# Block softmax attention: scores of both heads as float32 matmuls in the two row halves of the PE array, in rounds of two score tiles

## What is computed

```python
scale = D ** (-0.5)
q = (x @ Wq).reshape(B, S, H, D).transpose(0, 2, 1, 3)     # H = 16, D = 64
k, v = ...                                                 # the same with Wk, Wv
def step(carry, kv):                                       # over blocks of 64 keys
    o, m, l = carry
    kj, vj = kv
    s = jnp.einsum('bhnqd,bhkd->bhnqk', qb, kj) * scale
    m_new = jnp.maximum(m, s.max(axis=-1))
    p = jnp.exp(s - m_new[..., None])
    alpha = jnp.exp(m - m_new)
    l_new = alpha * l + p.sum(axis=-1)
    o_new = (alpha[..., None] * o + jnp.einsum('bhnqk,bhkd->bhnqd', p, vj)) / l_new[..., None]
    return ((o_new, m_new, l_new), None)
out = o.transpose(0, 2, 1, 3).reshape(B, S, H * D) @ Wo
x = x + out
```

## Time and profile before

| | |
|---|---|
| median of 3 runs | 3036.59 us |
| lowest, highest | 3035.76, 3037.22 us |
| the profiled execution: its time | 3035.88 us |
| its span in the trace | 3031.6 us |
| busy over the span: PE, DVE, ACT, POOL | 80%, 76%, 52%, 44% |
| the softmax attention, first projection to last addition | about 762 to 2552 us |

### The profile page before, as it was taken

One profiled execution on the slowest core, in us unless ns is written; L12 is line 12 of the kernel. 1 busy time (PEld: TensorE's weight loads), 2 busy tenths in 40 slices (PEclk: granted clock), 3 DMA queues, 4 the chain that ended last, 5 costly groups with the idle time before them and its releaser, 6 DMA issues. The chain is left out here.

```text
span 3031.6 us, 44901 instructions
## 1 busy us (share of the span) xinstructions
PE 2417.3 (80%) x15028; PEld 1802.3 (59%) x15028; DVE 2307.4 (76%) x4330; ACT 1571.3 (52%) x2571; POOL 1325.7 (44%) x893
## 2 busy tenths in 40 slices
PE   4985149951599999999999999999999996229980
PEld 2443148840377777777777777777777775218860
DVE  4535537754599999999998999999999996817762
ACT  2432123321377777777777777777777774113330
POOL 0001721135255555555555555555555554541117
PEclk8986579985699999999999999999999998559995
DMA  4240136642422323323233232232322310026652
GB/s 112 104 173 13 38 118 193 192 127 66 99 71 66 89 52 76 79 66 89 52 72 84 60 89 58 66 89 58 88 62 66 89 43 3 24 86 193 192 160 77
DMA packets 158617, 267.91 MB, mean 88 GB/s; under 512 B 30945, under 2 KB 105313, under 8 KB 158433
## 3 DMA queue, kind: packets, MB, share of 16 engines
q1 hardware_dynamic: 144048, 231.84, 28.9%
q0 software_dynamic: 8192, 16.79, 1.8%
q10 hardware_dynamic: 6192, 16.91, 1.4%
HBM read 120.83 MB, written 46.07 MB: 55 GB/s over the span
## 5 line engine op out<-in xcount | busy, mean ns | idle before, releaser
L1513 POOL TENSOR_TENSOR b_prob<-b_prob,b_weight 128x1024 f32<-128x1024 f32 x512 | 958.9, 1905 | 837.4 <-DVE b_weight L1489 837.4
L1452 DVE TENSOR_REDUCE b_bmax<-b_score 128x16 f32<-128x1024 f32 x512 | 621.4, 1214 | 89.7 <-PE b_score L1327 85.7
L1413 ACT ACTIVATE b_prob<-b_score,b_neg_m 128x1024 f32<-128x1024 f32 x512 | 570.9, 1115 | 170.5 <-DVE b_neg_m L1462 169.6
L1439 DVE TENSOR_REDUCE b_bsum<-b_prob 128x16 f32<-128x1024 f32 x512 | 618.8, 1209 | 0.0
L1403 ACT ACTIVATE b_pT<-b_turn 128x512 f32<-128x512 f32 x1024 | 555.4, 597 | 63.2 <-PE b_turn L1338 52.8
L1338 PE MATMUL b_turn<-ident,b_prob 128*128 128x128 f32 x4096 | 531.3, 273 | 1.0 <-ACT b_pT L1403 1.0
L1338 PEld LDWEIGHTS b_turn<-ident,b_prob 128*128 128x128 f32 x4096 | 477.8, 140 | 72.2 <-issue 3.2
L1327 PE MATMUL b_score<-b_KH,b_QS 128*128 128x512 f32 x1024 | 492.4, 481 | 23.4 <-issue 8.2
L1307 PE MATMUL b_acc<-b_pT,b_V 128*64 128x256 f32 x4096 | 498.5, 385 | 0.0
L1327 PE MATMUL b_score<-b_KL,b_QS 128*128 128x512 f32 x1024 | 406.0, 396 | 0.0
L1307 PEld LDWEIGHTS b_acc<-b_pT,b_V 128*64 128x64 f32 x4096 | 271.2, 136 | 154.0 <-issue 43.1
(11 more groups left out here) (196 smaller groups left out, 2706.9 us busy)
## 6 DMA issues: line engine op xcount, KB each, us to landing
f_e_w<-f_weights SPq DMA_DIRECT2D x80, 776.0 KB, 4.3
b_KH<-b_k_high SPq DMA_DIRECT2D x128, 256.0 KB, 4.4
b_KL<-b_k_low SPq DMA_DIRECT2D x128, 256.0 KB, 4.8
f_sorted<-a_zero ACTq DMA_DIRECT2D x43, 384.0 KB, 4.5
b_hb<-b_hT SPq DMA_DIRECT2D x32, 512.0 KB, 5.0
b_QS<-b_q_high SPq DMA_DIRECT2D x64, 256.0 KB, 3.5
b_QS<-b_q_low SPq DMA_DIRECT2D x64, 256.0 KB, 4.1
f_e_z<-f_sorted SPq DMA_DIRECT2D x82, 128.0 KB, 4.1
```

The source lines that it names most:

```text
L1413: act.activation(prob[r % 4][k][:], score[k % 2][:], ACT.Exp, bias=neg_m[r % 2][:, k:k + 1]).then_inc(prob_ready, 1)
L1439: dve.tensor_reduce(bsum[r % 2][:, k, :], prob[r % 4][k][:].rearrange("p (n c) -> p n c", c=KV_BLOCK), AX, ALU.add).then_inc(sum_ready, 1)
L1452: maxima = chain.mark(dve.tensor_reduce(bmax[r % 2][:, k, :], score[k % 2][:].rearrange("p (n c) -> p n c", c=KV_BLOCK), AX, ALU.max))
L1513: pool.tensor_tensor(tile, tile, weight[r % 2][:, k, :].unsqueeze(2).to_broadcast([P, NB, KV_BLOCK]), ALU.mult).then_inc(scaled, 1)
```

## The change

The scores become plain float32 matmuls with 64 rows: head 0 in partitions 0 to 63 and head 1 in 64 to 127, straight from the projection's own layout. So the split in high and low parts, its DVE instruction, the 12 DMAs of each pair and their semaphores go; ACT's copy of a projection (`qk_copy`) writes Q or K directly. The stream of each engine is no longer by tile but by **round** of two tiles (both heads of one query tile), rd = 0 and 1 in a slot:

```diff
+        Q = [sb(f"Q{i}", [P, SEQ]) for i in range(2)]
+        K = [sb(f"K{i}", [P, SEQ]) for i in range(2)]
+        def projected(j, r, rd, scores):
+            n, i = 2 * (r % GPP) + rd, 2 * j + r // GPP + 1
+            if not scores or i == PAIRS:
+                return None
+            if 1 <= n <= 4:
+                return "qk", i, i % 2, n - 1
+            if n >= 6:
+                return "v", i, i % 2, n - 6
+            return None
```

```diff
 PE
-                            if not (isinstance(sl, int) and sl == 0 and k < 2):
-                                pe.wait_ge(prob_ready, 4 * sl + k - 1)
-                            for c in range(2):
-                                for n, Kx in enumerate((KH, KL)):
-                                    last = pe.matmul(score[k % 2][:, c * HALF:(c + 1) * HALF], QS[par][h][:, q * P:(q + 1) * P],
-                                                     Kx[par][h][:, c * HALF:(c + 1) * HALF], start=n == 0, stop=n == 1)
-                            last.then_inc(scored, 1)
+                def score_round(j, r, rd):
+                    sl, par, q = 8 * j + r, r // GPP, (r % GPP) * QT + rd
+                    if rd == 0:
+                        pe.wait_ge(qk_taken, 4 * (2 * j + par) + 4)
+                    if sl or rd:
+                        pe.wait_ge(prob_ready, 4 * sl + 2 * rd)
+                    for c in range(2):
+                        for h in range(2):
+                            mine = slice(h * HD, (h + 1) * HD)
+                            last = pe.matmul(score[h][:, c * HALF:(c + 1) * HALF], Q[par][mine, q * P:(q + 1) * P],
+                                             K[par][mine, c * HALF:(c + 1) * HALF], start=True, stop=True)
+                    last.then_inc(scored, 2)
+                    for rd in range(2):
+                            score_round(j, r, rd)
+                        if rd == 1 and before:
+                            out_proj(g - 1, (gr - 1) % 8)
+                            turn_probs(g, gr, 2 * rd)
+                        if rd == 0 and before:
+                            pv(g - 1, (gr - 1) % 8, 2)
+                            pv(g - 1, (gr - 1) % 8, 3)
+                        if rd == 1 and finish:
+                            pv(g, gr, 0)
+                            pv(g, gr, 1)
+                        if finish:
+                            turn_probs(g, gr, 2 * rd + 1)
+                        made = projected(j, r, rd, scores)
```

```diff
 ACT, each round: oT copy (rd 1), two pT copies, two exponentials, two pT copies, rise (rd 0), projection copy
+                            for h in range(2):
+                                k = 2 * rd + h
+                                act.wait_ge(max_ready, 4 * sl + k + 1)
+                                act.activation(prob[r % 4][k][:], score[h][:], ACT.Exp,
+                                               bias=neg_m[r % 2][:, k:k + 1]).then_inc(prob_ready, 1)
 DVE
+                def maxima(sl, r, k):
+                    chain.link(dve.tensor_reduce(bmax[r % 2][:, k, :], score[k % 2][:].rearrange("p (n c) -> p n c", c=KV_BLOCK), AX, ALU.max))
+                    dve.tensor_reduce(neg_m[r % 2][:, k:k + 1], bmax[r % 2][:, k, :], AX, ALU.max, negate=True).then_inc(max_ready, 1)
+                    for rd in range(2):
+                            dve.wait_ge(scored, 4 * sl + 2 * rd + 2)
+                            for h in range(2):
+                                maxima(sl, r, 2 * rd + h)
+                        if rd == 0 and rest:
                             block_sums(n, nr, GT - 1)
+                            chain.link(dve.tensor_tensor_scan(flat(run_max), flat(first_low), flat(bmax[nr % 2]), 0.0, ALU.add, ALU.max))
...
+                        if rd == 0 and scores:
+                            block_sums(sl, r, 0)
...
+                        if rd == 1 and scores:
+                            block_sums(sl, r, 1)
+                            block_sums(sl, r, 2)
-                        made = projected(j, r, k, scores)
-                        if made and made[0] == "qk":
-                            low(made[1], made[3])
```

More of the change, by code:

```diff
@@ L1312, in slot, with out_proj @@
+                def out_proj(g, gr):
+                    misc_free()
+                    pe.wait_ge(o_ready, g + 1)
+                    hp = (g // GPP) % (HEADS // 2)
+                    for q in range(QT):
+                        last = pe.matmul(misc[:, q * D:(q + 1) * D], oT[gr % 2][:, q * P:(q + 1) * P], wo[:, hp, :],
+                                         start=True, stop=True)
+                    last.then_inc(wo_done, 1)
+                    last_use[0] = (wo_taken, g + 1)
                 def slot(j, r, scores, finish):
-                    sl, par = 8 * j + r, r // GPP
@@ L1445, in slot @@
-                    first = isinstance(sl, int) and sl == 0
-                    before = not (isinstance(sl, int) and sl <= LAG)
-                    rest = not first and (scores or r == 0)
+                    g, gr, before = sl - LAG, (r - LAG) % 8, sl > LAG
+                    rest = sl > 0 and (scores or r == 0)
                     n, nr = sl - 1, (r - 1) % 8
-                    for k in range(GT):
+                    for rd in range(2):
                         if scores:
-                            dve.wait_ge(scored, 4 * sl + k + 1)
-                            maxima = chain.mark(dve.tensor_reduce(bmax[r % 2][:, k, :], score[k % 2][:].rearrange("p (n c) -> p n c", c=KV_BLOCK), AX, ALU.max))
-                        if k == 0 and rest:
-                            m_i = chain.mark(dve.tensor_tensor_scan(flat(run_max), flat(first_low), flat(bmax[nr % 2]), 0.0, ALU.add, ALU.max))
-                        if k == 1 and rest:
-                            dve.wait_ge(rise_ready, n + 1)
-                            chain.wait(sums)
-                            scaled_sums = chain.mark(dve.tensor_tensor(flat(inv_l), flat(rise), flat(run_sum), ALU.mult))
-                        if scores:
-                            chain.wait(maxima)
-                            dve.tensor_reduce(neg_m[r % 2][:, k:k + 1], bmax[r % 2][:, k, :], AX, ALU.max, negate=True).then_inc(max_ready, 1)
-                        if k == 0 and rest:
@@ L1500, in _ @@
                 chain.link(dve.memset(last_one[:, :, NB - 1:NB], 1.0))
-                for u in range(4):
-                    low(0, u)
                 slots(dve, slot)
```

182 lines of the change are left out of this document (56 added, 126 removed).

## The result

The changed kernel takes 3074.85 us (median of 4 runs, 3073.34 to 3077.90) against 3036.47 for the kernel before on the same chip: a ratio of 1.0128 (95% interval 1.0110 to 1.0145), 38 us slower. The forecast was 3058, with 3022 to 3112 as its range and slower at 0.75. The profiled execution took 3074.61 us, of which its span is 3070.7, against 3031.6 before: 39.1 us to account for.

The account below looks back on a forecast made before the run. A DVE and POOL loop with the scan held in every slot was to bound it, with some PE lateness. Slots (13.80 - 13.57) x 127 = +29.2, start -9.3, end +2: +21.9, so 3058 us; range 3022 to 3112.

Parts of the forecast that it names:

- The loop of DVE and POOL: Weight, POOL, held scan, rest of DVE's stream, next weight: a floor of 13.7 us in all four slots.
- held until POOL is through: DVE's scan with two SBUF inputs waits for POOL's four multiplications, ending 0.14 us later, 8.00 us after the weight.
- PE late behind ACT's copy: PE's Wo product waits for ACT's copy of the V product: 0.1 to 0.2 us added in two slots of four.
- A score round: On PE, four matmuls with row halves side by side: 2.05 us, against 2.02 for two tiles before.
- B: PE's row halves run side by side but not freely: 0.3 to 0.5 us more a round, 3084 to 3121; chance 0.13.
- C: PE's row halves don't run together: 1.64 us more each round, slot about 16.7, 3426 us; chance 0.06.
- The start: Before the first scores: no deal and no low-part instructions, -9.8, less 0.5 for the exponential table: -9.3 us.
- the exponential table: At the start, the table would then be late, taking 0.5 us off the gain.
- The end: Last slots without scores do the same work; 2 us added for the last slot's longer chain.
- Rival D: DVE's scan isn't held for long, only PE binds: slot 13.2 to 13.3, 2989 us; chance 0.11.
- PE's bound: PE's work in a slot: 12.0 us plus 0.88 for each projection, 13.75 with two, 13.3 on average.
- Rival E: Links and overlaps cost less, or PE is never late: slot 13.6 to 13.65, 3033 to 3040 us; chance 0.10.

Follow-up runs that it names:

- number 1: Changed kernel with POOL weighting three of a slot's four tiles, so its part is 5.6 instead of 7.5 us: 3030.96 us, ratio 0.9982.
- number 5: Changed kernel plus an unused 512-element DVE reduction at the end of round 1, between weight and scan: 3065.57 us, ratio 1.0127.
- number 6: Changed kernel plus an unused 512-element DVE reduction in round 0, between scan and next weight: 3126.76 us, ratio 1.0327.
- number 8: Changed kernel with ACT's V-product copy ahead of the gap's exponential and PE's Wo product behind round 1's first transposes, scan unmoved: 3045.31 us, ratio 1.0059.
- number 10: Changed kernel's order by rounds with the split scores of the kernel before (parts, deal, DVE low part): 3099.97 us, ratio 1.0248.
- number 3: Changed kernel with a block sum ahead of the scan, ACT's V-product copy earlier and PE's Wo product behind the first transposes: 3019.49 us, ratio 0.9947.
- number 4: Kernel before with only the running-maximum scan moved behind the last block sum: 3008.61 us, ratio 0.9910.
- number 11: Kernel before with the scan behind the last block sum and projection steps placed as in the changed kernel: 2985.97 us, ratio 0.9872.
- number 2: Changed kernel with one block sum of DVE's round 0 moved ahead of the scan: 3088.22 us, ratio 1.0173.
- number 7: Changed kernel with a round's four score matmuls issued head by head instead of interleaved: 3065.10 us, ratio 1.0123.
- number 9: Kernel before, order by tile, with float32 scores straight from Q and K, one head at a time: 3510.08 us, ratio 1.1604.

## Why the prediction was right, and where its sum was off

- **The loop of DVE and POOL: right, nearly to the number.** From the weight's start the steps gave 8.00 for the scan's end, 8.38 for the clamp and 13.67 for the next weight; measured are 8.00, 8.38 and 13.73. Of the 0.06 us, 0.04 lie in the block sums and maxima (the addition to X starts at 12.26 for 12.22) and 0.02 between reciprocal and weight. Numbers 1, 5, 6 and 8 show that it is this loop, and number 8 shows it bare: 13.73 in all four slots. A scan that takes 0.28 us alone takes 1.76 when it is issued into POOL's work, so the port rule that I cited from the Trainium skill, SBUF - State Buffer, section SBUF: two separate sides, holds here. The scan's median is 1.09 and not near 1.7, because round 0's scores come 0.8 us late and use up part of the hold. As the step said, that costs nothing. One thing in the step is too broad: "held until POOL is through" is true only of a scan issued into POOL's last multiplication, from 6.00 us behind the weight on. In the last slot of the stage DVE has no maxima to take and comes earlier, and its three instructions with two SBUF inputs, behind the weight at 2551.17, are held one after the other:

```profile
2554.74 0.71 DVE L1434 TENSOR_TENSOR_SCAN b_run_max<-b_first_low,b_bmax 128x64 f32<-128x64 f32 x1
2555.48 1.76 DVE L1436 TENSOR_TENSOR b_run_max<-b_run_max,b_neg_m 128x64 f32<-128x64 f32 x1
2557.16 2.00 DVE L1438 TENSOR_TENSOR_SCAN b_run_sum<-b_first_zero,b_bsum 128x64 f32<-128x64 f32 x1
```

  They end 4.28, 6.07 and 7.99 us behind the weight. POOL's four multiplications, 7.49 us from 0.37 on, end at about 4.1, 6.0 and 7.9 if they are equally long: each held instruction waits for the multiplication at work, not for all of POOL's block.
- **PE late behind ACT's copy: right mechanism, somewhat too small.** I had 0.1 to 0.2 us in two slots, and measured 0.42 in one; that the mean comes out so near owes something to luck. The mean slot is 13.82 where 13.80 was forecast: +32.3 against +29.2. Number 8 shows that this lateness is the fourth slot's 0.42, since moving the copy takes it away.
- **A score round: cheaper than taken.** 1.92 us against 2.05. Rivals B and C fall by the changed kernel's own row: B wanted 0.3 to 0.5 us more, C 3.69 us in all. As the loop binds and not PE, the 0.13 us bought nothing.
- **The start: the failed step.** I gave -9.3 and measured +1.2, 10.5 us off. The scores did start earlier, by 10.2 us, a little more than the 9.8 worked out. The 0.5 us taken off for the exponential table is shown by no run: its load ends at 780.02, and ACT then waits 2.12 us for DVE. What I left out is how long the first weight then takes to come. A round's scores wait for both exponentials of the round ahead; with nothing else for PE to do, a round is a chain. In the rows above rounds start 7.5 to 7.9 us apart from the second on: 3.4 to 3.7 us of scores, then maxima and two exponentials. The tiles of before start 1.8 to 3.0 us apart in two buffers that take turns, 4.7 to 5.4 us for two. Number 10 gives the price of the rounds at the start, with the operands of before: 11.0 us from the first projection to the first weight (55.1 for 44.0), of which the direct operands give back 10.0. Part of the chain is the clock. The three rounds at 784.64, 792.53 and 800.07 ran at 0.50 to 0.56 and took 3.7, 3.5 and 3.4 us, where the same round takes 1.92 at 1.00, so an estimate from these figures is 4.8 us; ahead of them PE had stood idle for 4.08, 2.54 and 2.85 us. I had carried only the head start over and had no term for the speed of the work behind it.
- **The end: +2 was said, +3.9 measured.** It is the same kind of latency in the last slots: Wo product behind ACT's copy behind the exponential of the gap. Number 8, which takes the copy out of that place, ends 5 us sooner.
- **Rival D, the scan not held**, needed round 0's scores over 1.6 us late; they are 0.8 late. What it would give is shown by number 3, at 0.9947, where the scan is moved instead. My 2989 was too low for it: I had 13.2 to 13.3 for PE's bound, but with the float32 rounds it is 13.43 to 13.48 (numbers 1 and 3), though the round itself is cheaper. By the phases of number 3, the term that was too small is the transposes: I had 0.79 for eight, 3.50 in a slot with the 0.17 ahead of each product with V, and they take 3.89, 0.93 for eight even ahead of a projection (1502.34 to 1503.27). Projections are 1.45 where I had 1.32 for one and a half, Wo is 0.54 for 0.63, the scores 3.84 for 4.10, and the product with V is as said. Changing the form of the array may be in the projections' share; no run isolates it.
- **Rival E, about the same**: its condition that links and overlaps cost less isn't met; the loop costs 0.06 us more than said, and PE is late in one slot.

The change is slower because the order that its score form needs puts a held scan in every slot, where one slot in four had it. In that order the float32 operands are the better ones (number 10 against the change), but not by more than the order costs. The hold isn't the whole difference between the two forms, though: with it out of the way in both, the float32 form stands at 0.9947 (number 3) and the split form at 0.9910 (number 4, same chip) and 0.9872 (number 11), since PE then binds and the float32 rounds save it nothing.

Whether a scan with one operand in PSUM would escape the hold was not tried on the chip.

## What to carry to other kernels

A busy share of 92 to 97% on two engines didn't say which of them sets the period. The step between two marks of the same instruction, read slot by slot, did; and an instruction that is now and then several times longer than its size allows points at a loop to test. It is no proof: in number 3 one scan in four still takes 0.63 us, and PE is what binds. Put work that reads SBUF once, such as reductions, in front of a small two-input instruction that would be held, so that it falls behind POOL's end; the same work behind it is paid in full (numbers 5 and 6). But look at who else waits for that small instruction before moving it (number 2 lost where number 3 won). And when work is batched for the steady state, work out its latency once for the start and once for the end, without the neighbours that hide it.

## What I had not expected of the hardware

- Two row halves run side by side even if one head's matmuls are issued both ahead of the other's: a round of 1.93 us against 1.92, with records starting in pairs (number 7). The Trainium skill, TensorE: Matmul & The Clock Gate, section Part 3: Packing small matmuls - row/col tiling, says that matmuls start and end strictly in program order. By that, the second head's first matmul would have waited until the first head's second had begun, an estimated 0.9 us or more by the 1.91 that number 9 shows for two, and a round would be longer by as much; it grew by 0.01 us, so the measurement goes against a strict order of starts across the halves.
- A float32 score tile of one head takes 1.91 us, as long as the round of two heads (number 9).
- When the scan's hold ends depends on the POOL instruction at work and not on the scan's own issue: issued 6.24 us behind the weight it takes 1.76 us (number 8), issued at 7.13 it takes 0.87 (the changed kernel), and both end 8.00 us behind the weight. Issued at 3.57 it ends at 4.28 (the last slot of the changed kernel), behind the second of POOL's four.
